# One zeroed result row per token, filled by an adding scatter, in a Mamba and mixture-of-experts block

## The reference, cut to what matters

```python
shared = jnp.maximum(normed @ sw1 + sb1, 0.0) @ sw2 + sb2
probs = jax.nn.sigmoid(flat @ router_w.T)
scores, idx = jax.lax.top_k(probs, 2)              # two experts of eight
w = scores / (jnp.sum(scores, axis=-1, keepdims=True) + 1e-06)
comb = comb.at[jnp.arange(T)[:, None], idx].add(w)
h = jnp.maximum(jnp.einsum('td,edh->teh', flat, ew1) + eb1[None, :, :], 0.0)
eo = jnp.einsum('teh,eho->teo', h, ew2) + eb2[None, :, :]
routed = jnp.einsum('teo,te->to', eo, comb)
return shared + routed.reshape(b, s, -1)
```

## Time and profile before

| | |
|---|---|
| median of 3 runs | 1107.83 us (1104.26 to 1113.19) |
| the profiled execution's own time | 1108.14 us |
| its span, first to last instruction | 1106.3 us |
| busy over the span | PE 965.2, DVE 966.4, ACT 845.0, POOL 772.2 us |
| `RS` scatters (line 1860) | 92 instructions, 98.7 us busy, mean 1072 ns |
| `XS` scatters (line 1853) | 64 instructions, 66.0 us busy, mean 1031 ns |
| HBM read, written | 44.99 MB, 37.83 MB |

### The profile page before, as it was taken

One profiled execution on the slowest core, in us unless ns is written; L12 is line 12 of the kernel. 1 busy time (PEld: TensorE's weight loads), 2 busy tenths in 40 slices (PEclk: granted clock), 3 DMA queues, 4 the chain that ended last, 5 costly groups with the idle time before them and its releaser, 6 DMA issues.

```text
span 1106.3 us, 20653 instructions
## 1 busy us (share of the span) xinstructions
PE 965.2 (87%) x6072; PEld 549.6 (50%) x6072; DVE 966.4 (87%) x1769; ACT 845.0 (76%) x1604; POOL 772.2 (70%) x942
## 2 busy tenths in 40 slices
PE   5799999999999999999999999976888859999970
PEld 4345544544454455445444544532454527777750
DVE  6799999999999999999999999964788757888865
ACT  4799999999899999999998999964565625555540
POOL 2289899999989998887988788642545442666660
PEclk9899999999999999999999999986888969999995
DMA  5010321232232123000000000000001026777638
GB/s 148 17 27 14 127 81 71 81 139 78 71 111 98 70 77 142 4 3 5 3 8 4 4 3 4 5 1 0 31 29 39 27 86 200 232 218 227 223 101 228
DMA packets 57422, 83.93 MB, mean 76 GB/s; under 512 B 17562, under 2 KB 37664, under 8 KB 57312
## 3 DMA queue, kind: packets, MB, share of 16 engines
q1 hardware_dynamic: 52320, 74.13, 21.1%
q0 software_dynamic: 4992, 8.48, 2.3%
HBM read 44.99 MB, written 37.83 MB: 75 GB/s over the span
## 4 chain that ended last, share of the span: by engine, by line
PE 24%; ACT 19%; issue 10%; DVE 8%; DMA 2%; POOL 2%; SPq 0%; ACTq 0%; POOLq 0%; DVEq 0%
PE bank L688 3%; ACT E L957 2%; PE bank L689 2%; PE bank L690 2%; ACT xbc L1062 2%; PE bank L545 2%; PE bank L699 2%; PE bank L702 2%; PE bank L700 2%; PE bank L467 2%; ACT xtok L977 2%; ACT L1051 2%; ACT sqy L1025 1%; DVE M L1423 1%; DVE o_sb L1442 1%
## 5 line engine op out<-in xcount | busy, mean ns | idle before, releaser
L1407 DVE SCALAR_TENSOR_TENSOR cv<-bank,PAR,cv 128x511 f32<-128x511 f32 (+2 forms) x384 | 276.7, 741 | 4.4 <-ACT cv L969 1.0
L957 ACT ACTIVATE E<-bank 128x512 f32<-128x512 f32 x256 | 144.2, 603 | 45.6 <-PE bank L531 40.8
L1423 DVE SCALAR_TENSOR_TENSOR M<-E,bank 128x512 f32<-128x512 f32 x256 | 170.4, 677 | 1.2 <-ACT E L957 0.4
L1860 POOL DMA_INDIRECT RS<-y,XR x92 | 98.7, 1072 | 79.4 <-DVE y L1640 57.7
L467 PE MATMUL bank<-hn,WA 128*128 128x512 f32 x256 | 142.1, 637 | 3.8 <-DVE cv L1407 3.7
L1853 POOL DMA_INDIRECT XS<-stage,IDX x64 | 66.0, 1031 | 77.4 <-DVE run L1382 60.3
L1785 POOL TENSOR_TENSOR yt<-yt,ti 128x384 f32<-128x384 f32 x64 | 64.0, 1001 | 76.0 <-DVE ti L1480 76.0
L1154 ACT ACTIVATE hr<-bank,W1B 128x512 f32<-128x512 f32 x92 | 63.3, 688 | 57.1 <-PE bank L690 53.2
L1570 DVE TENSOR_TENSOR hL<-hr,hH 128x512 fp32r<-128x512 f32 x124 | 87.0, 702 | 4.3
L1731 POOL TENSOR_TENSOR dtx<-xtok,DTW 128x256 f32<-128x256 f32 x128 | 80.1, 626 | 12.9 <-ACT xtok L977 7.5
L1789 POOL TENSOR_TENSOR y<-yt,zs 128x512 f32<-128x512 f32 x64 | 82.1, 1282 | 5.0
(11 more groups left out here) (239 smaller groups left out, 2615.1 us busy)
## 6 DMA issues: line engine op xcount, KB each, us to landing
XS<-PADT SPq DMA_DIRECT2D x32, 520.0 KB, 4.9
W1B<-WD SPq DMA_DIRECT2D x23, 514.0 KB, 3.6
W2B<-WD SPq DMA_DIRECT2D x23, 512.5 KB, 4.9
WD<-WS SPq DMA_DIRECT2D x16, 512.0 KB, 2.9
XR<-XS SPq DMA_DIRECT2D x23, 260.0 KB, 4.4
RW<-w_in SPq DMA_DIRECT2D x18, 256.0 KB, 5.5
xin<-x_in SPq DMA_DIRECT2D x4, 512.0 KB, 8.1
PC<-p SPq DMA_DIRECT2D x128, 6.0 KB
```

Source lines behind the costliest of these rows:

```text
L957: f(E[i % 2][:, :], bank[2 + i % 2][:, :], ACT.Exp).then_inc(e_a, 1)
L1407: stt(out=cv[t][:, s:L], in0=src[:, 0:L - s], scalar=PAR[:, bass.ds(cw + 3 - s, 1)], in1=cv[t][:, s:L], op0=ALU.mult, op1=ALU.add).then_in ...
L1423: stt(out=M[i % 4][:, :].rearrange("p (n t) -> p n t", n=4), in0=E[i % 2][:, :].rearrange("p (n t) -> p n t", n=4), scalar=1.0, in1=bank[5 ...
L1860: nc.gpsimd.indirect_dma_start(RS[:, :], bass.IndirectOffsetOnAxis(ap=XR[i % XD][:, (c + 1) * ROW - 1:(c + 1) * ROW].bitcast(I32), axis=0) ...
```

## The change

`RS` gets one row for each token and 1024 rows that take the padding. SP writes zeros over the first 4096 rows, in four transfers of 512 KB in the steps 3 to 6. A padding row's number is now 4096 plus a number from 0 to 1023, so within a tile they are distinct, and padding rows are written too. Both of a token's results carry the same row number, and the scatter adds to what stands in memory. A token's two experts lie in different tiles, so POOL waits ahead of each tile until all four scatters of the tile before have landed. The last pass loads one tile for each sequence, and the first of DVE's three operations is gone.

```diff
-        RS = nc.dram_tensor("RS", [2 * NB * L, DM], F32, kind="Internal").ap()
+        RS = nc.dram_tensor("RS", [NB * L + 1024, DM], F32, kind="Internal").ap()
...
                     sp.wait_ge(padt_p, 2)
+                    if k < 3 + NB // 2:
+                        at = (k - 3) * 1024
+                        sp.dma_start(RS[at:at + 1024, :].rearrange("(p n) d -> p n d", p=P),
+                                     PADT[:, :].rearrange("p (n d) -> p n d", d=ROW)[:, :, 0:DM]).then_inc(zero_out, 16)
...
             for b in range(NB):
-                for part, dst in enumerate((RA, RB)):
-                    sp.dma_start(dst[b][:, :].rearrange("p (s d) -> p s d", s=4),
-                                 RS[part * CAP + b * L:part * CAP + (b + 1) * L, :].rearrange("(s p) d -> p s d", p=P)).then_inc(ra_in[b], 16)
+                sp.dma_start(RA[b][:, :].rearrange("p (s d) -> p s d", s=4),
+                             RS[b * L:(b + 1) * L, :].rearrange("(s p) d -> p s d", p=P)).then_inc(ra_in[b], 16)
...
-                dve.wait_ge(ra_in[b], 32)
-                tt(RA[b][:, :], RA[b][:, :], RB[b][:, :], ALU.add).then_inc(fin_sum, 1)
-                wait(dve, fin_sum, b + 1)
+                dve.wait_ge(ra_in[b], 16)
...
-            nc.gpsimd.iota(PADT[:, :]..., pattern=[[0, 8]], base=PAD, channel_multiplier=0).then_inc(padt_p, 1)
+            nc.gpsimd.iota(PADT[:, :]..., pattern=[[1, 8]], base=NB * L, channel_multiplier=8).then_inc(padt_p, 1)
...
-                nc.gpsimd.iota(rows[:, :, :, ROW - 1], pattern=[[P, 4], [CAP, 2]], base=n * L, channel_multiplier=1).then_inc(dest_p, 1)
+                nc.gpsimd.iota(rows[:, :, :, ROW - 1], pattern=[[P, 4], [0, 2]], base=n * L, channel_multiplier=1).then_inc(dest_p, 1)
...
+            pool.wait_ge(zero_out, 16 * (NB // 2))
             for i in range(NT):
                 pool.wait_ge(y_v, i + 1)
+                if i > 0:
+                    returned(pool, i - 1)
                 for c in range(4):
-                    wait(pool, rs_out[4 * (i % 2) + c], 16 * (i // 2))
                     nc.gpsimd.indirect_dma_start(
                         RS[:, :],
                         bass.IndirectOffsetOnAxis(ap=XR[i % XD][:, (c + 1) * ROW - 1:(c + 1) * ROW].bitcast(I32), axis=0),
-                        y[i % 2][:, c * DM:(c + 1) * DM], None, bounds_check=2 * CAP - 1, oob_is_err=False).then_inc(rs_out[4 * (i % 2) + c], 16)
+                        y[i % 2][:, c * DM:(c + 1) * DM], None, compute_op=ALU.add).then_inc(rs_out[4 * (i % 2) + c], 16)
```

More of the change, by code:

```diff
@@ L47 @@
 ROW = DM + 2
-PAD = 1 << 20
 WR = 2 * HE + 8
@@ L172, in build @@
         RA = [sb(f"RA{b}", L) for b in range(NB)]
-        RB = [sb(f"RB{b}", L) for b in range(NB)]
         def first_bank(n):
@@ L211, in build @@
         raw_in, split_p, unit_out, pad_out = [sem(n) for n in ("raw_in", "split_p", "unit_out", "pad_out")]
-        padt_p, iota_p = sem("padt_p"), sem("iota_p")
+        padt_p, iota_p, zero_out = sem("padt_p"), sem("iota_p"), sem("zero_out")
         s1_a, s1_v, fms_mm, mean_mm = sem("s1_a"), sem("s1_v"), sem("fms_mm"), sem("mean_mm")
@@ L224, in build @@
         ra_in = [sem(f"ra{b}_in") for b in range(NB)]
-        fin_sum, fin_gb, fin_o = sem("fin_sum"), sem("fin_gb"), sem("fin_o")
+        fin_gb, fin_o = sem("fin_gb"), sem("fin_o")
         def steps(eng, body):
@@ L1686, in _ @@
             pool.wait_ge(padt_p, 1)
-            nc.gpsimd.iota(PADT[:, :].bitcast(I32).rearrange("p (n d) -> p n d", d=ROW)[:, :, ROW - 1], pattern=[[0, 8]], base=PAD,
-                           channel_multiplier=0).then_inc(padt_p, 1)
+            nc.gpsimd.iota(PADT[:, :].bitcast(I32).rearrange("p (n d) -> p n d", d=ROW)[:, :, ROW - 1], pattern=[[1, 8]], base=NB * L,
+                           channel_multiplier=8).then_inc(padt_p, 1)
             def norm_apply(n):
```

## The result

The changed kernel takes 1183.63 us, median of four runs (1178.17 to 1187.21), against 1109.9 (1104.26 to 1113.19) before, run beside it: a ratio of 1.0666, 95% interval 1.06 to 1.0731. It is slower by 74 us; 1179 was forecast. The profiled execution is the slowest of the four, 1187.21 us, with a span of 1185.4.

What follows compares the result with a forecast made beforehand. PE bounded the expert stage at 6.82 us a tile; POOL's landing chain would replace it at 10.5. Span 1106.3 + 77.8 (stage) - 6.0 (last pass) = 1178.1, forecast 1179; own case 1150 to 1200, 53 in 100.

Steps and rivals of the forecast that it cites:

- start-up: Expert stage, POOL: from the release of the wait to the first scatter, 0.77 us paid for each tile.
- term 2: Expert stage, POOL: first to fourth scatter 4.25 us; adding descriptors taken as no difference, bounds 0 and +0.3 us each.
- Scatter instructions clearly over 1.0 us each: Expert stage, POOL: a sign named for the prediction being wrong, pointing to descriptors.
- fourth scatters that land in over 5 us: Expert stage: a sign for being right, with the last four tiles' landing in about 3 us.
- term 3: Expert stage: landing of a tile's fourth scatter, 4.7 us for 19 tiles, 2.3 for the last four, plus the addition.
- Again it is among the loads: Expert stage: the fourth scatter, at R + 5.0 after landing R, falls among weight loads from near R + 4 to R + 6.4.
- The lock to the landing: Expert stage: DVE's `weigh` waits for the landing two tiles back, PE's work behind it, so everything is locked to it.
- out of the crowd: Rival, expert stage: scatters fall between load bursts, landing 2.3 + 0.8 us everywhere, time 1134; 16 in 100.
- The addition's own data: Expert stage: reading each row before the write adds 0.8 us to a landing, between 0 and 2.4.
- The rival built on it: Expert stage: the second read doubles the data's share of landings, 50 us in place of 18, time 1211; 22 in 100.
- The clock: Rival, expert stage: idling PE loses clock; at 0.83 still hidden, at 0.50 throughout 55 us more, 1234; 3 in 100.
- DVE's chain of 17.1 us: Last pass: estimate by DVE's operations, beside 15.3 us plus some 2.5 of start by DMA engines; 17.6 was taken.

Runs made afterwards that it cites:

- run with two tables: Changed kernel with even and odd tiles adding into separate zeroed tables, POOL waiting two tiles back, last pass adding both tables: 1131.34 us, ratio 1.0209.
- wait-alone run: Kernel before with only POOL's wait, ahead of each tile, for the plain scatters of the tile before: 1143.37 us against 1108.54, ratio 1.0297.
- run with plain scatters: Changed kernel with the addition left out of the scatter, so rows are overwritten; waits, zeroing and short last pass stay: 1127.81 us, ratio 1.0194.
- the one with POOL's help: Kernel before with 2 KB pieces in the last pass and three of eight sequences summed on POOL: 1115.65 us, ratio 1.0047.

## Why the prediction was right

The time was right, 1179 for 1183.6, and so was the mechanism in its outline: a landing that two tiles of distance had hidden becomes part of each tile. But two terms of the sum were wrong by about 35 us each, in opposite directions, and cancelled. That the time came within 5 us is luck. Against the profiled execution:

| term | forecast | measured | difference in all |
|---|---|---|---|
| first `y` done | 928.1 | 933.4 | +5.3, not of the change |
| start-up | 0.77 | 0.80 | +1 |
| first to fourth scatter | 4.25 | 5.82 | +36 |
| landing of the fourth, 19 tiles | 4.7 + 0.8 | 3.7 | -35 |
| the same, last four tiles | 2.3 + 0.8 | 3.3 | +1 |
| last pass | 17.6 | 16.6 | -1 |

The first `y` is 934.17 - 0.77. The measured ones are means over the tiles named. The span came out at 1185.4 for 1178.1, and these terms give the 7.

**Descriptors (term 2).** "I take no difference" was the wrong end of a bounded term, and the bound itself, 0.3 us, was too low: the adding form takes 0.6 us longer, and the 92 instructions are 149.1 us busy instead of 98.7. The run with two tables shows it by itself: POOL waits for no landing, and it is 23 us slower. "Scatter instructions clearly over 1.0 us each" was one of the signs named for being wrong, and it came; "fourth scatters that land in over 5 us" was one for being right, and it did not (3.7).

**The crowd (term 3).** "Again it is among the loads" failed. The lock to the landing holds for DVE: in most tiles `weigh` starts 0.12 us behind it (at 1006.73 for 1006.61). But I carried the old distance from `weigh` to the `W1B` load, 4.05 us, over to a period in which PE idles. In the tile shown above PE and ACT have worked ahead while DVE waits, and `W1B` comes 1.2 us behind the start of `weigh`; in the tile before, 3.2. The crowd meets the first two scatters there, or the second and third, which nobody waits for last. That was the rival "out of the crowd", given 16 in 100. Its place for the fourth scatter was right, and its 1134 is too low mainly for the descriptors: 1134 + 36 + 5 is 1175, and 11 of the last 12 us up to the profiled 1187 are a landing of 3.7 in place of 3.1 in 19 tiles. One reading was off as well: the second scatter of the earlier trace rows had not landed when the loads were issued. It landed at 1040.19 + 2.2 = 1042.4, behind the issue of `W1B` and of `W2B`, and was not slowed by them. The wait-alone run shows how loose such a phase is: 2.2 to 5.3 us for the fourth landing, tile by tile.

**The addition's own data.** I took 0.8 us; the runs give 0.6 of longer instruction, which I had not counted there, and 0.4 to 0.5 for the data in quiet. The Trainium skill, Collectives: The Full Stack, "The bandwidth ceiling", has half the rate for a reducing collective because of the second read. The direction agrees; the size does not: 0.69 us of all 16 engines against 0.19, 3.7 times, with 144 packets a scatter in place of 32. The rival built on it would have made 1211; it failed because the crowd, in which the extra engine time would have hurt, was off the path. Even there its 2.1 + 2 x 2.6 = 7.3 us was not reached: the slowest of all 92 landings took 6.7.

**The clock.** It fell to 0.89 on the mean over the stage and stayed hidden, as the rival's first half said. In single stretches of 10 us it was between 0.66 and 1.00, where before it was 1.00 throughout; even so PE idles 46 of 210 us. That it cost nothing at all is argued from this and not tested.

**What was hidden stayed hidden.** Zeroing cost nothing (0.9998). The last pass gave 7.0 us for the forecast 6.0, since the DMA engines, at 0.84 and 235 GB/s, did not bind it; DVE's chain of 17.1 us was the better of the two estimates. Padding rows cost about 3 us, within the spread of the runs.

The parts don't add up singly: the wait alone +35, the adding alone +23, the last pass -5 make +53, and the change is +74. The traces say where the missing 21 us lie. From the end of the first `y` to the last landing it takes 154.6 us before (928.1 to 1082.7), 191.0 with the wait alone (928.1 to 1119.1), 177.1 with two tables and 235.4 in the changed kernel (933.4 to 1168.8). So behind the wait the adding costs 44 us, not 23. The 23 distances from first to fourth scatter grow by 37 of them (96.4 to 133.9 us in all), the 23 fourth landings by 8 (74.8 to 83.0). Without the wait, POOL's slack of 1.6 us a tile takes up much of the longer instructions; the wait uses up the same slack, and then they count in full. That is about 15 of the 21 us, and the later landing most of the rest.

## What to carry to other kernels

Before a wait is tightened from two steps back to one, add up instruction, landing and start-up of what is waited for against the period: in the run with plain scatters 0.8 + 3.8 + 2.2 was just the 6.8 us at hand, and with adding each further microsecond was paid 23 times. Slack can be spent once: two changes that each hide in it cost more together than the sum of both. Halving the bytes of a last pass was worth 5 to 7 us; an adding scatter cost POOL 0.6 us and the DMA engines 0.5 us each for it, 92 times, in a stage where POOL had 1.6 us of slack a tile. Work moved to an engine that had been done early also moves that engine's end: the last piece on POOL brought its drain of 8.2 us to the end of the launch. And do not carry the phase of a transfer over into a schedule with another bound: what was locked to an engine's work moves as soon as that engine begins to wait.

## What was not expected of the hardware

- An indirect scatter of 128 rows of 512 B with addition takes GpSimd 1.58 us to issue, without 0.96 to 0.98, whether its rows are written or not.
- It occupies the 16 DMA engines for 0.69 us instead of 0.19 (worked out above from the queue's share of the span), in 144 packets instead of 32.
- Two element-wise operations on SBUF tiles of 128 x 512 fp32, one on DVE and one on POOL at the same time, ran at 1.64 and 1.6 us; DVE's takes 0.69 with POOL idle.
- POOL's closing drain ended 8.2 us after its last instruction of work, a plain scatter in the kernel before and an element-wise operation in the one with POOL's help, and 5.9 us after the changed kernel's last adding scatter.
